# Another order for the first feed-forward step of a fused layer: five engines' lists rearranged

## What is computed

```python
x = x + _layernorm(attn_ref(_layernorm(x), ...))
x = x + _layernorm(ffn_ref(_layernorm(x), W1, b1, W2, b2))

# attn_ref(x)                              # ffn_ref(x)
uv = x @ in_proj_w + in_proj_b             # _ternary(w): scale = mean|w|
u, v = uv[..., :D], silu(uv[..., D:])      #   clip(round(w / scale), -1, 1)
v = dwconv(v, conv_w, conv_b)   # 3 taps   h = x @ _ternary(W1).T + b1   # 512 -> 2048
h_t = a * h_(t-1) + ssm_b * v_t # scan     h = gelu(h)
y = ssm_c * h + ssm_d * v                  out = h @ _ternary(W2).T + b2  # 2048 -> 512
out = (u * silu(y)) @ out_proj_w + out_proj_b
h = out + x
return layernorm(h) * ln_w + ln_b
```

## Time and profile before

| | us |
|---|---|
| median of 3 runs | 1434.34 (1433.7 to 1436.07) |
| the profiled execution | 1434.67 |
| its span, first to last instruction | 1432.4 |
| PE busy | 1402.3 (98%) |
| DVE / ACT / POOL busy | 1117.5 / 875.7 / 447.9 |
| mean granted clock of TensorE | 0.995 |

### The profile page before, as it was taken

How to read it: one execution, slowest core, us unless ns; L and a number is a source line. 1 busy time by engine, 2 the same in 40 slices (tenths; PEclk the granted TensorE clock), 3 DMA queues, 4 the chain that set the end, 5 groups by cost and what they waited for, 6 DMA issues and landing times.

```text
span 1432.4 us, 19035 instructions
## 1 busy us (share of the span) xinstructions
PE 1402.3 (98%) x6528; PEld 639.4 (45%) x6528; DVE 1117.5 (78%) x1892; ACT 875.7 (61%) x1261; POOL 447.9 (31%) x518
## 2 busy tenths in 40 slices
PE   7898999999999999999999999999999999999997
PEld 4343444444444444444444444444444444444443
DVE  7997996867878677796877968678786877998734
ACT  7897666656756466565656756566565655753443
POOL 4244242330514224142331523315132241322221
PEclk9999999999999999999999999999999999999999
DMA  8712311221213113121221113122121131001200
GB/s 232 247 51 64 84 59 30 65 53 31 68 21 89 30 30 89 24 66 30 52 67 30 61 29 89 30 30 81 22 75 30 45 74 30 30 1 30 59 30 30
DMA packets 155984, 82.00 MB, mean 57 GB/s; under 512 B 132720, under 2 KB 132720, under 8 KB 155760
## 3 DMA queue, kind: packets, MB, share of 16 engines
q1 hardware_dynamic: 155888, 80.79, 22.1%
HBM read 31.49 MB, written 16.78 MB: 34 GB/s over the span
## 4 chain that ended last, share of the span: by engine, by line
PE 87%; DVE 7%; issue 3%; DMA 2%; POOL 1%; ACT 0%; SPq 0%; DVEq 0%; ACTq 0%; POOLq 0%
PE f2b L580 14%; PE f1b L551 14%; PE f2b L581 14%; PE f1b L552 14%; PE misc L519 6%; PE misc L517 6%; PE misc L518 6%; PE misc L533 3%; PE misc L531 3%; PE misc L532 3%; DVE bn L775 1%; DMA stage<-w_in_dram 1%; DMA xs<-x_dram 1%; DVE vl L851 0%; DVE yb L890 0%
## 5 line engine op out<-in xcount | busy, mean ns | idle before, releaser
L580 PE MATMUL f2b<-w,ring 128*128 128x512 fp8e5 x1008 | 382.3, 379 | 1.0 <-DVE ring L793 1.0
L581 PE MATMUL f2b<-w,ring 128*128 128x512 fp8e5 x1008 | 382.4, 379 | 0.0
L551 PE MATMUL f1b<-x3T,w 128*128 128x512 f16 x960 | 365.0, 380 | 7.2 <-ACT ring L1587 7.1
L552 PE MATMUL f1b<-x3T,w 128*128 128x512 f16 x960 | 365.1, 380 | 0.0
L1587 ACT ACTIVATE ring<-f1b,par 128x512 f32<-128x512 f32 x256 | 174.9, 684 | 235.4 <-PE f1b L552 230.4
L2008 POOL TENSOR_SCALAR ve<-mv 128x4 f32<-128x4 f32 (+2 forms) x88 | 35.5, 403 | 699.1 <-DVE mv L785 698.9
L793 DVE SCALAR_TENSOR_TENSOR ring<-ring,f_sc 128x512 f16<-128x512 f32 x256 | 211.8, 841 | 40.8 <-ACT ring L1597 40.6
L1597 ACT ACTIVATE ring<-ring,f_sc 128x512 f16<-128x512 f32 x256 | 179.7, 710 | 0.0
L517 PE MATMUL misc<-x1T,win_hi 128*128 128x512 f16 x456 | 173.0, 379 | 0.0
L518 PE MATMUL misc<-x1T,win_hi 128*128 128x512 f16 x456 | 173.0, 379 | 0.0
L519 PE MATMUL misc<-x1T,win_lo 128*128 128x512 f16 x456 | 172.9, 379 | 0.0
(11 more groups left out here) (219 smaller groups left out, 2049.5 us busy)
## 6 DMA issues: line engine op xcount, KB each, us to landing
out_dram<-hb SPq DMA_DIRECT2D x64, 256.0 KB, 2.0
xs<-x_dram SPq DMA_DIRECT2D x14, 1024.0 KB, 5.6
ring<-w1t_dram SPq DMA_DIRECT2D x3, 1024.0 KB, 12.6
stage<-w2t_dram SPq DMA_DIRECT2D x3, 1024.0 KB, 8.4
x1T<-tp SPq DMA_TRANSPOSE x68, 3.1
xs<-x_dram SPq DMA_DIRECT2D x4, 256.0 KB, 3.6
stage<-w_in_dram SPq DMA_DIRECT2D x4, 256.0 KB, 6.1
xs<-x_dram SPq DMA_DIRECT2D x2, 512.0 KB, 7.6
```

What stands on the lines that cost most here:

```text
L551: pe.matmul(b[:, :], w, src[:, k, :], start=k == 0, stop=False)
L552: mm = pe.matmul(b[:, :], w, src[:, KC + k, :], start=False, stop=k == KC - 1)
L580: pe.matmul(f2b[q][:, :], h_hi[:, i % H_SLOTS, qs], w2[:, j, :], start=j == 0, stop=False)
L581: mm = pe.matmul(f2b[q][:, :], h_lo[:, i % H_SLOTS, qs], w2[:, j, :], start=False, stop=j == FC - 1)
```

## The change

The table `ORDER` gives the chunks other numbers, `SIGNED` follows, and the calls of the first step stand in another order on PE, DVE, ACT and GpSimd. No call is added or dropped, and SyncE's program is the same. The diff, cut to its core:

```diff
-ORDER = [(W1_CHUNK, 0), (W1_CHUNK, 2), (W1_CHUNK, 3), (W1_CHUNK, 1), (W1_CHUNK, 7), (W1_CHUNK, 5), (W1_CHUNK, 6), (W1_CHUNK, 4),
...
+ORDER = [(W1_CHUNK, 0), (W1_CHUNK, 2), (W1_CHUNK, 3), (W1_CHUNK, 1), (W1_CHUNK, 5), (W1_CHUNK, 6), (W1_CHUNK, 10), (W1_CHUNK, 9),
...
@@ tensor
             f1(0, 4)
+            f2(0, 0)
             f1(0, 5)
             f1(0, 6)
             f1(0, 7)
-            f2(0, 0)
+            f2(0, 1)
             f1(0, 8)
-            f2(0, 1)
+            f2(0, 2)
             f1(0, 9)
-            f2(0, 2)
+            f2(0, 3)
             f1(0, 10)
-            f2(0, 3)
+            f2(0, 4)
             o(1, 0)
             o(1, 1)
             o(1, 2)
-            f2(0, 4)
             o(1, 3)
...
@@ scalar
-            residual(1, 0)
-            centre_tap(2, 0)
...
-            sign_w1(3)
...
             gelu(0, 9)
             sign_w2(2)
+            sign_w1(3)
...
@@ gpsimd
             keep_state(1, 2)
+            add_bias(1, 0)
             keep_state(1, 3)
-            add_bias(1, 0)
             add_bias(1, 1)
+            add_bias(1, 2)
             rstd_x(3)
-            add_bias(1, 2)
             add_bias(1, 3)
```

More of the change, by code:

```diff
@@ L671, in _ @@
             transpose_x3(3)
+            in_proj("u", 1, 2, u_mm, range(0, 2))
             threshold(1)
-            in_proj("u", 1, 2, u_mm, range(0, 2))
             transpose_x3(4)
@@ L710, in _ @@
             f2(0, 9)
+            in_proj("v", 3, 2, v_mm)
+            f2(0, 10)
             f1(0, 15)
-            f2(0, 10)
-            in_proj("v", 3, 2, v_mm)
             f2(0, 11)
@@ L1391, in _ @@
             gate_lo(1, 3)
-            x_stats(3, 0)
-            ternary(16)
+            ternary(17)
+            ternary(18)
+            ternary(19)
+            x_stats(3, 1)
             aggr(0, 3, 0)
-            x_stats(3, 1)
             x_stats(3, 2)
@@ L1401, in _ @@
             aggr(0, 3, 3)
-            ternary(17)
-            lo(0, 4)
+            lo(0, 5)
+            lo(0, 6)
+            h_add(1, 1)
             h_stats(1, 0)
-            h_add(1, 1)
-            lo(0, 5)
+            h_stats(1, 1)
             aggr(1, 1, 0)
[L1408 to L1411, removed]
             ternary(20)
             h_add(1, 2)
+            ternary(21)
+            ternary(22)
+            h_stats(1, 2)
+            h_add(1, 3)
             t_lo("t1", 3, 0)
-            ternary(21)
             aggr(1, 1, 1)
-            h_add(1, 3)
-            h_stats(1, 2)
-            ternary(22)
             h_stats(1, 3)
@@ L1423, in _ @@
             aggr(1, 1, 3)
+            ternary(24)
+            t_lo("t1", 3, 1)
             lo(0, 7)
-            t_lo("t1", 3, 1)
-            ternary(24)
             lo(0, 8)
@@ L1464, in _ @@
             lo(0, 12)
-            lo(0, 13)
             ternary(28)
+            ternary(29)
             second_norm(N3, 0)
@@ L1472, in _ @@
             t_lo("t3", 1, 1)
-            ternary(29)
-            lo(0, 14)
+            lo(0, 13)
             t_lo("t3", 1, 2)
             ternary(30)
+            lo(0, 14)
             t_lo("t3", 1, 3)
@@ L1864, in _ @@
             gelu(0, 0)
+            sign_first(0)
+            hi(0, 0)
+            copy_u(2)
             gelu(0, 1)
-            sign_first(0)
-            sign_first(2)
[L1868 to L1880, removed]
+            d_conv(1, 0)
+            hi(0, 1)
+            gelu(0, 2)
+            sign_first(1)
+            copy_u(3)
+            gelu(0, 3)
+            d_conv(1, 1)
+            hi(0, 2)
+            sign_first(3)
+            d_conv(1, 2)
+            gelu(0, 4)
+            residual(1, 0)
+            d_conv(1, 3)
+            gelu(0, 5)
+            centre_tap(2, 0)
+            sign_w2(1)
+            gelu(0, 6)
+            sign_first(2)
             hi(0, 3)
[L1882 to L1885, removed]
             gelu(0, 7)
@@ L1901, in _ @@
             centre_tap(2, 3)
-            hi(0, 4)
+            residual(1, 2)
             hi(0, 5)
-            residual(1, 2)
+            residual(1, 3)
             hi(0, 6)
-            sign_w1(3)
[L1907 to L1910, removed]
             gelu(0, 9)
             sign_w2(2)
+            sign_w1(3)
+            norm_x(3, 0)
+            t_hi("t1", 3, 0)
+            hi(0, 7)
             gelu(0, 10)
+            norm_x(3, 1)
+            hi(0, 8)
             norm_x(3, 2)
-            hi(0, 7)
             t_hi("t1", 3, 1)
             t_hi("t1", 3, 2)
-            hi(0, 8)
+            hi(0, 9)
             gelu(0, 11)
@@ L1921, in _ @@
             t_hi("t1", 3, 3)
-            hi(0, 9)
+            gelu(0, 12)
             hi(0, 10)
             hi(0, 11)
-            gelu(0, 12)
             gelu(0, 13)
+            silu_v(3, 0)
             hi(0, 12)
+            silu_v(3, 1)
             gelu(0, 14)
-            silu_v(3, 0)
             hi(0, 13)
+            sign_w2(3)
+            silu_v(3, 2)
             hi(0, 14)
-            sign_w2(3)
-            silu_v(3, 1)
-            silu_v(3, 2)
             t_hi("t3", 1, 0)
```

60 lines of the change are left out of this document (32 added, 28 removed).

## The result

The changed kernel takes 1425.55 us (median of 4 runs, 1424.9 to 1427.28) beside 1434.37 us for the kernel before (4 runs, 1433.7 to 1436.07): a ratio of 0.9942, 95% interval 0.993 to 0.9955. In a second comparison, of 5 runs with 15, it is 1425.05 and 1433.93, ratio 0.9944 (0.9931 to 0.9956). The forecast was 1426.1.

A forecast was written before the change was run, and what follows sets the result against it. PE bounds the kernel, its one large wait caused by the late W1 reload; 8.74 us gained, less 0.35 and 0.15, gives 8.25, so 1434.34 - 8.25 = 1426.1 us, range 1425.0 to 1428.4.

The forecast's parts named there:

- the hole of 8.74 us: PE before f1(0, 11), held by the late W1 reload: 7.23 us of waiting and 1.51 of slow clock.
- Part 1: W1's reload: ternary(19) ends at 124.5 instead of 130.8, gelu(0, 9) leaves its path; the 7.23 us and slow clock go.
- The sum: Whole kernel: 8.74 gained, less 0.35 for ternary(14), less 0.15 of a possible 0 to 0.75: 8.25 us.
- Part 2: f1(0, 12) next waits for DVE's ternary(21 to 24): 0 to 0.3 us stay, to 1.1 with two more blocks.
- The rival B: First-half holes of 1.3 to 4.3 us from more GpSimd blocks or a 3.75 us copy; 1426.9 to 1429.9; chance 0.16.
- the forecast: Case A, whole kernel: 0 to 1.3 us of waits stay, 1425.6 to 1426.9 us; chance 0.75.
- Part 3: PE's earlier f2s: f2(0, 2) waits 0.35 us for ternary(14); gelu(0, 8) is in time for f1(0, 10) by 0.4.
- Part 4: centre_tap(2, 0) waits for GpSimd's keep_state(1, 0): copy takes 1.09 us, no ACT wait; at 3.08, ACT waits 0.6.
- The rule of the Trainium skill: Against the copy at keep_state(1, 0): two-SBUF-input VectorE instructions and GpSimd SBUF reads contend, the second blocking fully, scans included.
- Part 5: Second half: two more table loads, 1.28 us each; 0.4 us spare before the last silu_v, another 0.7 behind.
- The gain passes to the end: Behind f1(1, 0) at 179.03: PE's other waits are 1.3 us in all, lists are the old ones.

The follow-up runs named there:

- the second trace: The changed kernel unaltered, run again for another trace and more times: 1425.05 us against 1433.93 before.
- The run with one column: The changed kernel with GpSimd's four add_bias calls of tile 1 adding the bias to one column of 512 only: 1425.86 us, ratio 0.994.
- the fourth: The changed kernel unaltered, traced once more after two repeats: 1426.94 us, stretch 87.23 us.
- the gelu-last kernel: The changed kernel with gelu(0, 9) put back behind sign_w1(3) on ACT, all else as changed: 1426.86 us, ratio 0.9949.

## Why the prediction was right, and where it was not

**What bounded the kernel, and the hole of 8.74 us.** Right. Moving three ternaries in the old order returned 7.80 of it; moving the gelu returned nothing.

**Part 1, the reload.** The sum had 0.5 us for one block by GpSimd and put the issue at 124.5, 39.0 behind the start of `transpose_x3(0)`. Without the two blocks it is 38.9 (125.33 in the second trace), with them 40.9 (125.14 in the first). What it lacked are these two: it looked for `add_bias(1, 0)` ahead of `ternary(19)` and not for `add_bias(1, 1)` and `(1, 2)`, which came there as well. `add_bias(1, 0)` cost what it said: `ternary(16)` took 1.10 us, 0.36 more than its neighbours. The price of the other two, taken from the earlier trace rows as 0.4, was mis-sized. There GpSimd's call, 119.84 to 121.24, ran beside a statistic for most of its time, and the ternary at 120.64 lost only the rest of it. A call that gets in just as a two-input operation begins costs 1.0. `gelu(0, 9)` was ready in all courses.

**Part 2, what is late next.** `f1(0, 12)` is late by 0.26 where 0 to 0.3 stood. But that was not the first place. The step that failed, in three of the four traces, is the list of what stands behind the four ternaries: the part counts `h_add(1, 0)` among DVE's work and does not ask who waits for it. By the prediction's own numbers it would have been plain. `f1(0, 11)` at 134.02, and 0.35 later for `f2(0, 2)`, is 134.37; `o(1, 2)` stands 32 matmuls, 6.90 us, before it, so it is due at 127.47. `h_add(1, 0)` ends 2.71 behind the start of the first statistic (125.04 to 127.75 in the trace), and the first statistic starts 0.08 before the end of `ternary(19)` at 124.5, so that is 127.13. The margin was 0.3 us, and each block on DVE ahead of it goes straight to PE. The rival B named GpSimd's blocks and a stretch of 1.3 to 4.3 us of holes; the three traces with some 2.3 us of holes (0.36 + 1.67 + 0.26) are this rival, the one with 0.35 is the forecast. By the stretch alone these are 1434.34 - 6.45 = 1427.9 us and 1425.9. That both are one kernel, the prediction did not see.

**Part 3.** Right: `f2(0, 2)` waits 0.35 to 0.36, against 0.35; `f1(0, 10)` waits for nothing.

**Part 4.** Right in size and place: the first copy took 1.10 us, ACT did not wait before the centre_tap. DVE's two scans and GpSimd's copy in the changed kernel:

```profile
102.10 2.46 DVE L860 TENSOR_TENSOR_SCAN vl<-a_par,carry,vl 128x512 f32<-128x512 f32 x2
...
103.44 1.10 POOL L2059 COPY carry<-vl 128x1 f32<-128x1 f32 x1 [17.26 <-DVE vl L860]
```

The reason was half of it. The copy doesn't get in *while* a scan runs: with the scans apart it took 0.19 us, so of the 1.10 some 0.9 are standing beside the second scan, and of the 1.76 of the run with a ternary between some 1.6, beside a ternary and a scan. It gets in where a scan *ends* (103.44 + 1.10 = 104.54, the scan at 104.56), though a two-input operation follows at once. The rule of the Trainium skill that stood against this step ("SBUF — State Buffer", section "Who interferes with whom") isn't contradicted: two-input operations of DVE do keep GpSimd out as it says (`add_bias(1, 1)` 3.94 us in place of 1.3), and so, by the lengths of the copies, does a scan. What the prediction took for a contradiction is the change from a scan to the operation behind it, where the waiting call had its turn each time in these lists, while a row of other two-input operations mostly passed it by.

**Part 5.** Right. Between 138.7 and `f1(1, 0)` no call of PE is late, and the two table loads cost PE nothing.

**The sum.** 8.25 forecast; 6.46, 8.42, 6.45 and 6.29 in the four traces. The medians say 8.82 and 8.88, more than the traces with blocks. The interval of the ratio reaches from 6.3 to 9.9 us, and the start of a run, which differs by up to 3.4 us with the same calls, may have a part in the 8.82. That the median came within 0.6 us of the forecast is therefore partly luck. An estimate says which course the runs without a trace took: the shortest start (83.49), the shortest rest (1253.8) and the 2.1 us between span and time give at least 1426.5 with the blocks and 1424.5 without; five of the seven took 1424.72 to 1425.05. (The run with one column, which has no blocks, came 0.9 under its 1424.5 once, so the bound with blocks may be 1425.6.) So most of them were probably of the course without blocks, in which the sum was right within 0.2 us.

**Behind `f1(1, 0)`.** "The gain passes to the end" holds but for a few tenths: two `f1`, at 430 and 949 us, wait for a transfer, 0.35 us together in the trace of before and 0.78 to 1.25 in the twelve others. The run of the gelu alone in the old order (0.93) is among them, so it isn't the new order that makes this.

**What stays open.** What decides at that boundary: the order of the starts in the records does not. Whether the long start of the second trace has a part in its course: an edited kernel shows the unblocked stretch with a short start, but it can't meet that boundary, and the one with the scans apart, where GpSimd stood with a start of 84.25, has another list on DVE. The start of a run varies in part with PE's clock: PE waits for 2.7 to 3.7 us until 56 to 58 us, and from 58 to 62 the granted clock was 0.88 to 1.00 in the three traces with the shortest starts (83.5) and 0.50 in the four with the longest (86.0 to 86.9), which is the half level. This is PE by stretch in the second trace of the changed kernel (start 86.44) and in the fourth (83.50):

```profile
58.00:62.00 4.00, 4.00 (x11) 0.50 0.21 42
...
58.00:62.00 4.00, 4.00 (x20) 1.00 0.26 51
```

Why it drops in one run and not in another, the traces don't show.

## What to carry to other kernels

When a stall comes from a transfer that waits for work on another engine, look for the few calls that it waits for before you look at the whole order: three calls gave 7.80 of the 8.4 us here. After taking a stall away, list for each engine who waits for every call behind the edit, and its margin; the margins of a few tenths are where contention turns into time. And when one trace of a kernel disagrees with a forecast by an amount that a pair of blocks explains, take a second trace: the same code may have two courses.

## What the hardware showed

- The same GpSimd operation of 512 columns takes 1.27 to 1.30 us beside statistics or when it gets in first, and 3.94 or 6.48 when DVE runs operations with two SBUF inputs back to back; one of one column takes 0.19 or 2.50 in the same way.
- When it gets in, a two-input DVE operation that begins 0.08 to 0.09 us behind it takes 1.75 or 1.76 instead of 0.74 us; one that began 0.38 behind it took 1.44.
- A one-column copy takes 0.19 us where DVE had left a gap of 0.03 us (one run), 1.10 beside a scan and 1.76 beside a ternary and a scan, and ends within 0.02 us of the scan's record.
- Of five traces in which GpSimd's record starts 0.08 to 0.09 us before that of a two-input operation (the gelu-last kernel's among them), four ended in GpSimd's favour and one in DVE's; of three with 0.18 to 0.24, one and two.
